# Third scores ahead of the out projection and the turning of h, in 29 of 64 steps of a transformer kernel

## The chip, the cores and the metric

The kernel runs on one core of a Trainium2 chip. The metric is the device time of one execution in microseconds (us), as the median of three executions. Five engines run their own instruction streams and meet at semaphores: TensorE (PE, its weight loads shown apart as PEld), VectorE (DVE), ScalarE (ACT), GpSimd (POOL) and SyncE (SP), which issues most of the DMAs.

## The reference

The input is 16 sequences of 256 tokens with 128 channels. A modulated layer norm and a wavelet mixer with linear attention come first; then four transformer layers, each with attention (16 query heads on 4 key heads, head size 64, causal) and a mixture of 8 experts of which every token uses two:

```python
for l in range(L):                       # L = 4
    res = x
    h = _rms(x, ln1_w[l])
    h = _attention(h, wq[l], wk[l], wv[l], wo[l], cos, sin, causal_bias)
    x = jnp.clip(res + h, -100.0, 100.0)
    res = x
    h = _rms(x, ln2_w[l])
    h = _moe(h, wr[l], wg[l], wu[l], wd[l])
    x = jnp.clip(res + h, -100.0, 100.0)
```

Inside `_attention`: q and k are projected and rotated by position, scores are scaled and masked, a softmax follows, the probabilities weigh v, and `wo` projects the result out.

## The kernel before, in words

After a prologue of some 243 us the kernel runs 64 **steps**, one for each sequence in each layer (16 sequences, 4 layers), and ends with the experts of the last eight sequences. A step `it` works on three sequences at once: attention of `it`; the rest of the attention, the out projection and the routing of `it - 1`; and the norm and the q and k projections of `it + 1`. The experts run in blocks of eight sequences, cut into 42 half steps, which are laid into the eight **places** (0 to 7) of later steps. Steps 0 to 8 have none at any place. In each later group of eight, the steps with remainder 0 and 7 have none, the step with remainder 1 has them at places 4 to 7 only, and the one with remainder 6 at places 0 to 5; the others have all eight. So place 3 is empty in steps 0 to 9, 15 to 17, 23 to 25, 31 to 33, 39 to 41, 47 to 49, 55 to 57 and 63: 29 steps, called light steps here. In all of them place 2 is empty too.

Nothing schedules at run time. Each engine's order is written out by hand in a loop over the steps, and the loops of PE and DVE have to name the same order, since they share PSUM banks. In a light step, between places 1 and 3, it is:

- PE: `scores(it, 1)` (L759), `attend(it - 1, 3)` (transposes L784, then the products with v, L802 and L804), `project_v(it)` (L841), `project_out(it - 1)` (L852), `turn_h(it + 1)` (L817, two transposes of the normed rows z), `scores(it, 2)` (L759), and after place 3 `project_qk(it + 1)` for outputs 0 and 1 (L832 to L834), `turn_routed(it - 1)` (L861) and output 2. After place 4 come `attend(it, 0)`, `route_logits` (L870), `scores(it, 3)`, outputs 3 and 4, `attend(it, 1)`, `route_ranks`.
- DVE: `mask_and_max(it, 1)`, `invert(it, 0)`, `copy_o(it - 1, 3)` (L1606), `update_x(it - 1)` (L1612, L1615), `low_h(it + 1)` (L1585), `mask_and_max(it, 2)` (four heads, each L1591 and L1593, then L1597), `invert(it, 1)` (L1602), `rope(it + 1)` for outputs 0 to 2 (L1572, two for each).
- ACT: `exps(it, 1)` (L1055), `copy_v`, `scale_rows(it + 1)`, `square_routed(it - 1)` (L1077), `copy_h(it + 1)` (L1072, L1073), `scale_routed`, and later `exps(it, 2)` behind `copy_logits`.
- POOL: `scatter(it - 2)` (L1299), `root`, `normalise(it, 0)` (L1308), `root_routed(it - 1)`, `normalise(it, 1)`, `low_piece`, `rope_adds` of outputs 0 to 2 (L1323), `normalise(it, 2)`.

`normalise(it, q)` divides the exponentials of the group of heads `q` after DVE's `invert`; `attend(it, q)` waits for it. `rope_adds` waits for a DMA that SP issues after `rope`.

**Banks.** Scores, out projection and q and k projections take turns in a ring of four PSUM banks (the S ring), numbered by `number_slots` in PE's order. A product may start when the slot four before it has been read:

```python
at_least(pe, "s_free", S_AT["out", it] - S_RING + 1)   # in project_out
```

`project_out` waits for this and, ahead of it, for `copy_o` of the last group. `project_qk` waits for `h_lo_ready` and for its own slot.

The chain that the new sequence's h takes is: out projection done, `update_x`, squares on ACT, `copy_h` on ACT (behind the squares in ACT's order), `low_h` on DVE, `project_qk`.

Of the kernel before, what the change touches and what calls it, by code (L numbers as in the profile page):

```python
# [128 lines left out]
def number_slots(half_steps):  # L129

    s, t, u = {}, {}, {}

    def moe(b, hs):
        m = hs // 2
        g = b * PT + m
        if hs % 2 == 0:
            if m < PT:
                u["rows", g] = len(u)
            if m > 0:
                u["gated", g - 1] = len(u)  # L140
        else:
            if m < PT:
                u["gate", g, 0] = len(u)
                u["gate", g, 1] = len(u)
            if m > 0:
                t["y", g - 1] = len(t)

    def place(it, p):
        if (it, p) in half_steps:
            moe(*half_steps[it, p])  # L150

    def scores(it, q):
        for i in range(4):
            s["head", it, q, i] = len(s)

    def attend(it, q):
        for i in range(4):
            t["probs", it, q, i] = len(t)
        u["o", it, q] = len(u)

    def qk(it, outputs):
        for m in outputs:
            s["qk", it, m] = len(s)

    for it in range(-1, NIT + 1):
        now, coming, old = 0 <= it < NIT, it + 1 < NIT, it >= 1
        if now:
            scores(it, 0)
        place(it, 0)
        if old:  # L170
            attend(it - 1, 2)
        place(it, 1)
        if now:
            scores(it, 1)
        if old:
            attend(it - 1, 3)
        if now:
            t["v", it] = len(t)
        place(it, 2)
        if old:  # L180
            s["out", it - 1] = len(s)
        if coming:
            t["h", it + 1] = len(t)
        if now:
            scores(it, 2)
        place(it, 3)
        if coming:
            qk(it + 1, range(2))
        if old:
            t["routed", it - 1] = len(t)  # L190
        if coming:
            qk(it + 1, range(2, N_QK1))
        place(it, 4)
        if now:
            attend(it, 0)
        if old:
            t["logits", it - 1] = len(t)
        place(it, 5)
        if now:
            scores(it, 3)  # L200
        place(it, 6)
        if coming:
            qk(it + 1, range(N_QK1, N_QK))
        if now:
            attend(it, 1)
        if old:
            t["ranks", it - 1] = len(t)
        place(it, 7)
    for hs in range(HS):
        moe(NB - 1, hs)  # L210
    return s, t, u


def bass_program(nc, I, out):
    ctx = ExitStack()
    with ctx:
# [207 lines left out]
        half_steps = half_step_places()  # L424
# [251 lines left out]
        def _(pe):  # L676
# [268 lines left out]
            def place(it, p):  # L945
                if (it, p) in half_steps:
                    moe(*half_steps[it, p])

            phase_done(pe, 0)
            for it in range(-1, NIT + 1):  # L950
                now, coming, old = 0 <= it < NIT, it + 1 < NIT, it >= 1
                if now:
                    scores(it, 0)
                place(it, 0)
                if old:
                    attend(it - 1, 2)
                place(it, 1)
                if now:
                    scores(it, 1)
                if old:  # L960
                    attend(it - 1, 3)
                if now:
                    project_v(it)
                place(it, 2)
                if old:
                    project_out(it - 1)
                if coming:
                    turn_h(it + 1)
                if now:
                    scores(it, 2)  # L970
                place(it, 3)
                if coming:
                    project_qk(it + 1, range(2))
                if old:
                    turn_routed(it - 1)
                if coming:
                    project_qk(it + 1, range(2, N_QK1))
                place(it, 4)
                if now:
                    attend(it, 0)  # L980
                if old:
                    route_logits(it - 1)
                place(it, 5)
                if now:
                    scores(it, 3)
                place(it, 6)
                if coming:
                    project_qk(it + 1, range(N_QK1, N_QK))
                if now:
                    attend(it, 1)  # L990
                if old:
                    route_ranks(it - 1)
                place(it, 7)
# [374 lines left out]
        def _(dve):  # L1368
# [235 lines left out]
            def copy_o(it, q):  # L1604
                u_is_full(dve, ("o", it, q))
                V.tensor_copy(oT[:, 2 * q:2 * q + 2, :].rearrange("p a b -> p (a b)"), psum[:, u_bank(("o", it, q)), :]) \  # L1606
                    .then_inc(sem("u_free"), 1)
# [100 lines left out]
            def place(it, p):  # L1708
                if (it, p) in half_steps:
                    moe(*half_steps[it, p])  # L1710
# [3 lines left out]
            for it in range(-1, NIT + 1):  # L1714
                now, coming, old = 0 <= it < NIT, it + 1 < NIT, it >= 1
                if now:
                    mask_and_max(it, 0)
                if old:
                    invert(it - 1, 3)
                place(it, 0)  # L1720
                if old:
                    copy_o(it - 1, 2)
                if coming and it + 1 >= B:
                    combine(it + 1)
                place(it, 1)
                if now:
                    mask_and_max(it, 1)
                    invert(it, 0)
                if old:
                    copy_o(it - 1, 3)  # L1730
                place(it, 2)
                if old:
                    update_x(it - 1)
                if coming:
                    low_h(it + 1)
                if now:
                    mask_and_max(it, 2)
                    invert(it, 1)
                place(it, 3)
                if coming:  # L1740
                    rope(it + 1, range(N_QK1))
                place(it, 4)
                if now:
                    copy_o(it, 0)
                if old:
                    choose(it - 1)
                place(it, 5)
                if now:
                    mask_and_max(it, 3)
                    invert(it, 2)  # L1750
                place(it, 6)
                if coming:
                    rope(it + 1, range(N_QK1, N_QK))
                if now:
                    copy_o(it, 1)
                if old:
                    route(it - 1)
                place(it, 7)
# [58 lines left out]
```

How the kernel before makes its waits and increments, by code:

```python
        def phase_done(eng, k):  # L410
            eng.wait_ge(sem("phase_end"), PH * (k + 1))
# [1 line left out]
        def at_least(eng, name, n):  # L414
            if n > 0:
                eng.wait_ge(sem(name), n)
# [19 lines left out]
        def s_is_full(eng, key):  # L437
            eng.wait_ge(sem("s_full"), S_AT[key] + 1)
# [1 line left out]
        def t_is_full(eng, key):  # L440
            eng.wait_ge(sem("t_full"), T_AT[key] + 1)
# [1 line left out]
        def u_is_full(eng, key):  # L443
            eng.wait_ge(sem("u_full"), U_AT[key] + 1)
# [1 line left out]
        def s_was_read(eng, key):  # L446
            eng.wait_ge(sem("s_free"), S_AT[key] + 1)
# [1 line left out]
        def t_was_read(eng, key):  # L449
            eng.wait_ge(sem("t_free"), T_AT[key] + 1)
# [1 line left out]
        def u_was_read(eng, key):  # L452
            eng.wait_ge(sem("u_free"), U_AT[key] + 1)
# [34 lines left out]
        @block.sync  # L488
# [19 lines left out]
            def load_wv(l):  # L508
                load(wv, I["wv"][l], "wv_in")
            def load_wo(l):
                load(wo, I["wo_blocks"][l].rearrange("(c p) n -> p c n", p=P), "wo_in")
            load_wv(0)
            load_wo(0)
            load(wr, I["L0_ffn_wr"].rearrange("l h n -> h l n"), "wr_in")
            sp.wait_ge(sem("zeros_ready"), 1)
            for rows in rows_in + rows_out:
                for q in range(ZERO_PIECES):
                    sp.dma_start(zero_piece(rows, q), zeros).then_inc(sem("rows_zeroed"), 16)
            for h in range(2):
                sp.wait_ge(sem("x1_ready"), h + 1)
                sp.dma_start(x1_kept[:, half(h), :], x1[:, half(h), :]).then_inc(sem("x1_stored"), 16)
            def load_piece(it):
```

## Time and profile before

| | us |
|---|---|
| median of 3 executions | 3266.18 |
| lowest, highest | 3264.12, 3277.45 |
| the profiled execution | 3285.71 |
| its span, first to last instruction | 3283.9 |

In the profiled execution PE is busy for 80% of the span, DVE 67%, ACT 61%, POOL 57%. The mean granted TensorE clock is 0.919 of full speed: it stands at one of two levels, 1.2 or 2.4 GHz. Steps without expert work take 35.3 to 41 us, steps with it at all places 46.7 to 50 us. Times in rows are counted from the start of the span; "[x <-y]" behind a row is the idle time of its engine before it and what ended it. Matmuls are recorded as two instructions each where the operands are f32.

### The profile page before, as it was taken

The page shows a single profiled execution, that of the slowest core. Times are in us where ns is not written, and L with a number is a line of the kernel's source. Part 1 is how long each engine was busy: PE and PEld are TensorE (multiplying, and loading weights), DVE is VectorE, ACT ScalarE, POOL GpSimd, SP SyncE. Part 2 cuts the span into 40 slices and gives each one's busy share as a digit, 9 for nine tenths or more (in the row PEclk, how much of TensorE's full clock was granted, in tenths as well). Part 3 has the DMA queues.
Part 4 walks back from the last instruction along what each step waited for, and adds up shares of the span by engine and source line. Part 5 has one row for each costly group of instructions (what it writes and reads, how often), then busy time and mean ns, then how long its engine had stood idle before and what let it go on. Part 6 is the DMA issues. An engine that isn't in the chain of part 4 may idle for free.

```text
span 3283.9 us, 66162 instructions
## 1 busy us (share of the span) xinstructions
PE 2618.0 (80%) x20406; PEld 2095.5 (64%) x20406; DVE 2207.6 (67%) x8164; ACT 1996.6 (61%) x7080; POOL 1861.3 (57%) x1662
## 2 busy tenths in 40 slices
PE   5317887898889987899789987898889978998572
PEld 2316666777667766777667766777677766776462
DVE  6686676666777667776676767677676666765343
ACT  3017677667667666666666766676666766666220
POOL 0026676545666667655765666566766576555403
PEclk9659999999999999999999999999999999999665
DMA  9211122556246642654256633654266624652574
GB/s 373 118 46 65 68 78 86 181 177 198 71 161 212 206 137 80 222 192 154 77 189 228 212 106 116 201 194 139 74 214 218 200 76 145 201 193 89 164 240 128
DMA packets 287022, 511.54 MB, mean 156 GB/s; under 512 B 39969, under 2 KB 159297, under 8 KB 286145
## 3 DMA queue, kind: packets, MB, share of 16 engines
q1 hardware_dynamic: 270288, 473.72, 42.6%
q0 software_dynamic: 16384, 33.59, 3.3%
q8 instruction: 167, 2.74, 0.4%
q14 instruction: 183, 1.49, 0.2%
HBM read 316.58 MB, written 106.69 MB: 129 GB/s over the span
## 4 chain that ended last, share of the span: by engine, by line
PE 43%; DVE 19%; ACT 12%; POOL 11%; issue 7%; SPq 3%; another core or an unknown queue 3%; DMA 2%; DVEq 0%; POOLq 0%
PE psum L784 6%; PE psum L802 6%; DVE arena L1572 5%; ACT arena L1055 4%; PE psum L759 4%; PE psum L852 4%; POOL arena L1308 4%; ACT arena L1063 3%; PE psum L804 3%; POOL arena L1275 2%; DVE arena L1593 2%; PE psum L902 2%; PE psum L832 2%; POOL rows_in L1299 2%
## 5 line engine op out<-in xcount | busy, mean ns | idle before, releaser
L1055 ACT ACTIVATE arena<-arena 128x128 f32<-128x128 f32 (+1 forms) x2048 | 902.3, 446 | 53.4 <-DVE arena L1597 47.5
L1308 POOL TENSOR_TENSOR arena<-arena 128x512 f32<-128x512 f32 (+1 forms) x512 | 743.6, 1472 | 208.4 <-DVE arena L1602 208.3
L1323 POOL TENSOR_TENSOR arena<-arena 128x512 f32<-128x512 f32 x320 | 401.6, 1282 | 491.6 <-DMA arena<-arena 491.3
L784 PE MATMUL psum<-arena 128*128 128x128 f32 x3072 | 478.1, 294 | 225.5 <-ACT arena L1063 154.9
L1063 ACT COPY arena<-psum 128x384 f32<-128x384 f32 x1024 | 447.5, 482 | 312.7 <-PE psum L784 217.4
L784 PEld LDWEIGHTS psum<-arena 128*128 128x128 f32 x3072 | 347.5, 147 | 341.0 <-ACT arena L1063 214.5
L759 PE MATMUL psum<-arena 64*128 64x128 f32 (+1 forms) x4096 | 419.8, 342 | 12.7 <-DVE arena L1593 7.0
L1593 DVE CUSTOM_DVE_ANT_0 arena<-psum,arena 128x256 f32<-128x256 f32 x1024 | 429.3, 419 | 0.0
L1606 DVE COPY arena<-psum 128x512 f32<-128x512 f32 x256 | 176.4, 689 | 347.3 <-PE psum L804 314.2
L1572 DVE TENSOR_TENSOR arena<-psum,arena 128x512 f32<-128x512 f32 x640 | 390.8, 675 | 1.9 <-PE psum L834 1.8
L1055 ACT ACTIVATION_READ_ACCUMULATOR arena<-arena 128x1 f32 x2048 | 389.9, 190 | 0.0
L802 PE MATMUL psum<-arena 128*64 128x256 f32 x2048 | 355.3, 428 | 35.7 <-DVE xT_lo L1683 30.2
L759 PEld LDWEIGHTS psum<-arena 64*128 64x128 f32 x4096 | 301.3, 190 | 55.7 <-issue 26.2
L1591 DVE CUSTOM_DVE_ANT_0 arena<-psum,arena 128x128 f32<-128x128 f32 x1024 | 292.4, 286 | 31.3 <-PE psum L759 17.0
L1299 POOL DMA_INDIRECT rows_in<-arena x256 | 259.4, 1013 | 75.3 <-issue 69.3
L852 PE MATMUL psum<-arena 128*128 128x128 f32 x2048 | 247.3, 279 | 27.6 <-issue 27.5
L852 PEld LDWEIGHTS psum<-arena 128*128 128x128 f32 x2048 | 240.3, 196 | 37.0 <-issue 36.5
L832 PE MATMUL psum<-h_hi,wqk_hi 128*128 128x256 f32 x640 | 197.1, 308 | 69.2 <-DVE arena L1593 52.6
L804 PEld LDWEIGHTS psum<-arena 128*64 128x64 f32 x2048 | 160.3, 150 | 91.6 <-issue 26.7
L1275 POOL DMA_INDIRECT arena<-rows_out,arena x192 | 189.1, 985 | 52.3 <-issue 52.3
L804 PE MATMUL psum<-arena 128*64 128x128 f32 x2048 | 215.1, 290 | 0.0
L1689 DVE SCALAR_TENSOR_TENSOR arena<-arena,psum 128x512 f32<-128x512 f32 x160 | 108.0, 675 | 149.2 <-ACT arena L1138 122.9
(199 smaller groups left out, 5440.5 us busy)
## 6 DMA issues: line engine op xcount, KB each, us to landing
gu<-gu_kept SPq DMA_DIRECT2D x320, 512.0 KB
wd<-wd_kept SPq DMA_DIRECT2D x320, 256.0 KB
arena<-arena SPq DMA_DIRECT2D x128, 384.0 KB, 3.0
arena<-arena SPq DMA_DIRECT2D x128, 256.0 KB
arena<-rows_in SPq DMA_DIRECT2D x320, 64.0 KB
rows_out<-arena SPq DMA_DIRECT2D x320, 64.0 KB
rows_in<-arena SPq DMA_DIRECT2D x34, 512.0 KB, 8.0
rows_out<-arena SPq DMA_DIRECT2D x34, 512.0 KB, 7.1
```

Source lines behind the costliest of these rows:

```text
L759: return T.matmul(psum[:, s_bank(("head", it, q, i)), cols], QKT[par][r, 2 + 2 * q + i // 2, rows * P:(rows + 1) * P], QKT[par][r, q // 2, ...
L784: mm = T.transpose(psum[:, t_bank(key), j * P:(j + 1) * P], probs[:, q, i, j * P:(j + 1) * P], ident)
L802: return T.matmul(psum[r, bank, c0:c0 + S], v[:, 0, kv], pt[:, 0:S], start=True, stop=False, skip_group_check=True)
L804: return T.matmul(psum[r, bank, c0 + P:c0 + S], v[:, 1, kv], pt[:, S:S + P], start=False, stop=True, skip_group_check=True)
L852: mm = T.matmul(psum[:, s_bank(("out", it)), t * P:(t + 1) * P], oT[:, c, t * P:(t + 1) * P], wo[:, c, :], start=(c == 0), stop=(c == NH / ...
L1055: ins = A.activation(a, a, ACT.Exp, bias=negmax[:, q, k:k + 1], accum_out=rowsum[:, q, k:k + 1])
L1063: A.copy(probsT[:, 4 * (q % 2) + i, :], psum[:, t_bank(key), 0:3 * P]).then_inc(sem("t_free"), 1)
L1299: G.indirect_dma_start(rows_in[b % 2], bass.IndirectOffsetOnAxis(place_of[:, it % B * ST + t, j:j + 1], 0), z2[:, it % 2, t, :], None).the ...
L1308: ins = G.tensor_tensor(a, a, r[:, :, t:t + 1].broadcast_to([P, 4, P * (t + 1)]), ALU.mult)
L1323: G.tensor_tensor(keys_and_queries(it, u), keys_and_queries(it, u), turned_part[:, u, :], ALU.add) \
L1572: return V.tensor_tensor(dst.rearrange("p (i s) -> p i s", i=2), psum[:, s_bank(("qk", it, u)), :].rearrange("p (i s) -> p i s", i=2), tab ...
L1593: V.tensor_tensor_reduce(probs[:, q, i, P:3 * P], psum[:, s_bank(key), P:3 * P], mask, SCALE, -3.0e38, ALU.add, ALU.max, rowmax[:, q, 2 * ...
```

## The change

In the three places that set the order (the numbering of the slots, PE's loop and DVE's loop), steps whose place 3 is empty get `scores(it, 2)` before `project_out(it - 1)` and `turn_h(it + 1)`. On DVE `mask_and_max(it, 2)` and `invert(it, 1)` come before `update_x(it - 1)` and `low_h(it + 1)`. Steps with expert work at place 3 keep their order. ACT, POOL and SP keep theirs everywhere. No instruction is added or removed.

```diff
@@ number_slots @@
+        free = (it, 3) not in half_steps
+        if now and free:
+            scores(it, 2)
         if old:
             s["out", it - 1] = len(s)
         if coming:
             t["h", it + 1] = len(t)
-        if now:
+        if now and not free:
             scores(it, 2)
@@ TensorE's loop @@
+                free = (it, 3) not in half_steps
+                if now and free:
+                    scores(it, 2)
                 if old:
                     project_out(it - 1)
                 if coming:
                     turn_h(it + 1)
-                if now:
+                if now and not free:
                     scores(it, 2)
@@ VectorE's loop @@
                 if old:
                     copy_o(it - 1, 3)
+                free = (it, 3) not in half_steps
+                if now and free:
+                    mask_and_max(it, 2)
                 place(it, 2)
+                if now and free:
+                    invert(it, 1)
                 if old:
                     update_x(it - 1)
                 if coming:
                     low_h(it + 1)
-                if now:
+                if now and not free:
                     mask_and_max(it, 2)
                     invert(it, 1)
```

PE in a light step, from the v projection to the first q and k projection, before (`L852` is the out projection, `L817` the turning of h, `L759` the scores):

```order
L841 MATMUL psum<-arena 128x256 x2
L852 MATMUL psum<-arena 128x128 x16
L817 MATMUL psum<-arena 128x128 x2
L759 MATMUL psum<-arena 128x128 x2
L759 MATMUL psum<-arena 128x256 x2
L759 MATMUL psum<-arena 128x128 x2
L759 MATMUL psum<-arena 128x256 x2
L832 MATMUL psum<-h_hi,wqk_hi 128x256
```

and after (every line number is 3 higher):

```order
L844 MATMUL psum<-arena 128x256 x2
L762 MATMUL psum<-arena 128x128 x2
L762 MATMUL psum<-arena 128x256 x2
L762 MATMUL psum<-arena 128x128 x2
L762 MATMUL psum<-arena 128x256 x2
L855 MATMUL psum<-arena 128x128 x16
L820 MATMUL psum<-arena 128x128 x2
L835 MATMUL psum<-h_hi,wqk_hi 128x256
```

The eight products of the third scores left the place between `turn_h` and `project_qk`, where nothing stands now, and stand ahead of the out projection.

DVE at the same place, from `copy_o` (L1606) on, before; L1612 and L1615 are `update_x`, L1585 `low_h`, and the mask of the first head follows:

```order
L1606 COPY arena<-psum 128x512
L1612 TENSOR_TENSOR arena<-arena,psum 128x256
L1615 TENSOR_SCALAR arena<-arena 128x256
L1585 TENSOR_TENSOR h_lo<-arena,h_hi 128x256
L1591 ISA arena<-psum,arena 128x128
```

and after, the end of that piece (line numbers 6 higher): the last head's mask, the negation L1603, `invert` L1608, `update_x`, `low_h`, and at once `rope` (L1578):

```order
L1599 ISA arena 128x1
L1603 TENSOR_SCALAR arena<-arena 128x8
L1608 RECIPROCAL arena<-arena 128x8
L1618 TENSOR_TENSOR arena<-arena,psum 128x256
L1621 TENSOR_SCALAR arena<-arena 128x256
L1591 TENSOR_TENSOR h_lo<-arena,h_hi 128x256
L1578 TENSOR_TENSOR arena<-psum,arena 128x512 x6
```

The whole third mask moved from behind `low_h` to before `update_x`.

## Rows read from the trace of the kernel before

**Rows 1.** The page: busy time and share of each engine; the chain that ended last.

```profile
PE 2618.0 (80%) x20406; PEld 2095.5 (64%) x20406; DVE 2207.6 (67%) x8164; ACT 1996.6 (61%) x7080; POOL 1861.3 (57%) x1662
...
PE 43%; DVE 19%; ACT 12%; POOL 11%; issue 7%; SPq 3%; another core or an unknown queue 3%; DMA 2%; DVEq 0%; POOLq 0%
```

**Rows 2.** Timeline of step 4: start us, length us, engine, line, operation, operands, count.

```profile
398.92 0.69 DVE L1606 COPY arena<-psum 128x512 f32<-128x512 f32 x1 [3.28 <-PE psum L804]
...
399.71 3.81 PE L852 MATMUL psum<-arena 128*128 128x128 f32 x32 [0.68 <-issue]
...
403.36 0.38 PE L817 MATMUL psum<-arena 128*128 128x128 f32 x2
403.56 0.42 DVE L1612 TENSOR_TENSOR arena<-arena,psum 128x256 f32<-128x256 f32 x1 [3.95 <-PE psum L852]
...
403.67 1.58 PE L759 MATMUL psum<-arena 64*128 64x128 f32 x16
...
404.94 0.45 ACT L1072 ACTIVATE h_hi<-psum,arena 128x256 fp32r<-128x256 f32 x1
...
405.79 0.42 DVE L1585 TENSOR_TENSOR h_lo<-arena,h_hi 128x256 fp32r<-128x256 f32 x1 [1.48 <-ACT arena L1073]
406.13 0.28 DVE L1591 CUSTOM_DVE_ANT_0 arena<-psum,arena 128x128 f32<-128x128 f32 x1
...
406.68 0.08 DVE L1593 DVE_READ_ACCUMULATOR2_ANT arena<- 128x1 f32 x1
...
406.91 0.36 PE L832 MATMUL psum<-h_hi,wqk_hi 128*128 128x256 f32 x1 [1.66 <-DVE arena L1593]
...
408.66 1.83 DVE L1572 TENSOR_TENSOR arena<-psum,arena 128x512 f32<-128x512 f32 x3
```

**Rows 3.** Timeline of the end of step 4: POOL, and then PE in step 5.

```profile
415.86 3.77 POOL L1323 TENSOR_TENSOR arena<-arena 128x512 f32<-128x512 f32 x3 [2.35 <-DMA arena<-arena]
419.57 2.92 POOL L1308 TENSOR_TENSOR arena<-arena 128x512 f32<-128x512 f32 x2
...
422.55 0.66 PE L784 MATMUL psum<-arena 128*128 128x128 f32 x4 [0.17 <-POOL arena L1308]
```

**Rows 4.** Timeline of PE and DVE in step 3, the out projection and what ran before.

```profile
359.49 1.13 PE L841 MATMUL psum<-arena 128*128 128x256 f32 x4
362.75 5.44 PE L852 MATMUL psum<-arena 128*128 128x128 f32 x32 [2.13 <-issue]
...
361.95 0.69 DVE L1606 COPY arena<-psum 128x512 f32<-128x512 f32 x1 [4.24 <-remote]
```

**Rows 5.** Windows: stretch, length, busy PE, PEld, DVE, ACT, POOL, granted clock (PEclk), DMA share, GB/s; 6 us from `project_qk`'s start.

```profile
371.58:377.58 6.00, 5.76 (x50) 4.80 (x50) 5.40 (x21) 2.88 (x6) 4.09 (x3) 1.00 0.00 0
2702.81:2708.81 6.00, 4.60 (x35) 3.85 (x36) 5.33 (x20) 2.58 (x7) 4.81 (x5) 1.00 0.09 22
```

**Rows 6.** Windows, 6 us behind PE waits of 2.61, 3.00 and 2.42 us.

```profile
283.45:289.45 6.00, 5.76 (x47) 4.61 (x48) 0.77 (x2) 5.16 (x22) 2.68 (x4) 1.00 0.00 0
857.42:863.42 6.00, 5.75 (x32) 3.79 (x32) 3.88 (x24) 4.59 (x19) 4.87 (x6) 0.72 0.12 45
1302.28:1308.28 6.00, 5.77 (x32) 3.81 (x32) 3.84 (x23) 5.12 (x21) 4.85 (x6) 0.72 0.11 44
```

**Rows 7.** Windows, 6 us from the out projection's start, behind waits of 2.13 and 2.09 us.

```profile
362.75:368.75 6.00, 6.00 (x40) 5.83 (x42) 0.49 (x2) 1.02 (x3) 2.23 (x2) 0.72 0.01 3
508.85:514.85 6.00, 5.54 (x50) 4.92 (x50) 0.71 (x2) 2.44 (x9) 2.78 (x4) 1.00 0.00 0
```

**Rows 8.** Timeline of PE, outputs 3 and 4 and `attend(it, 1)`, in steps 3 and 40.

```profile
380.38 0.36 PE L832 MATMUL psum<-h_hi,wqk_hi 128*128 128x256 f32 x1 [0.85 <-DVE arena L1593]
...
383.80 0.65 PE L802 MATMUL psum<-arena 128*64 128x256 f32 x4
...
1998.81 0.44 PE L832 MATMUL psum<-h_hi,wqk_hi 128*128 128x256 f32 x1 [2.95 <-DVE arena L1593]
...
2003.73 0.65 PE L802 MATMUL psum<-arena 128*64 128x256 f32 x3
```

**Rows 9.** Windows of whole steps: 11 and 13 (experts at all places).

```profile
661.06:709.10 48.04, 43.97 (x353) 36.04 (x352) 31.77 (x125) 32.70 (x118) 23.71 (x21) 0.96 0.56 187
757.07:803.94 46.87, 42.58 (x352) 35.10 (x351) 31.56 (x125) 32.57 (x117) 23.72 (x21) 1.00 0.59 192
```

## The prediction, made before the changed kernel ran

> **What bounds the kernel now.** I read the page first, for the balance of the engines: PE is the busiest with 80% of the span and holds 43% of the chain that ended last, but DVE, ACT and POOL hold 42% of it together [rows 1]. So no engine is full; the work passes from hand to hand, and a change of order counts by what it does to the chain in a step. Then I read the timeline of a light step at full clock, step 4 [rows 2]. PE waits for `copy_o` of the last group of heads (DVE, 398.92), starts the out projection at 399.71, turns h until 403.36 + 0.38 = 403.74, and does the third scores (403.67, 1.58 us) while h goes from `update_x` (403.56) over ACT (404.94) to `low_h` (405.79 + 0.42 = 406.21). `project_qk` starts at 406.91, 1.66 us after the scores ended. What it waited for last is not h but a bank: output 0's slot is four behind the third scores' first head, and DVE masks that head only behind `low_h`, from 406.13 to 406.68 + 0.08. The windows were read last, for the granted clock behind such waits.
>
> **The change, term by term.** 29 steps change; steps 0 and 63 lack a neighbour, so 27 full ones count. Nothing is added or removed, so every term is a matter of place.
>
> *The start of the out projection.* Its slot now stands four behind the third scores' first head. Hence it waits for `copy_o` and for DVE to mask that head behind it. The mask of one head takes 406.76 - 406.13 = 0.63 us, and PE starts 0.15 us behind it, at 406.91 [rows 2]. Before, PE followed `copy_o` by 0.1 us; now by some 0.75. Cost: +0.65 us in each step. The scores themselves fit into PE's idle time ahead: 0.68 us of it in step 4 [rows 2], 2.13 in step 3 [rows 4], so in steps like 4 their first result comes at the earliest some 0.9 us after the v projection and the mask starts about 0.3 later. I take +0.65 to +0.95.
>
> *The start of `project_qk`.* The h chain keeps its length, since `update_x` finds DVE free: the third mask (2.5 us) and `invert` are over before the 3.81 us of the out projection are. But behind `low_h` nothing is left to wait for: the slot four before is the third scores' second head, long read. PE can start at about 406.25 instead of 406.91 [rows 2]: -0.66. The two terms cancel: 0 to +0.3 us a step, I take +0.15, which is +4 us for 27 steps.
>
> *`rope` of outputs 0 to 2.* DVE began it at 408.66 because mask and `invert` came before [rows 2]. Now it can follow output 0 directly, about 0.83 us (seven spacings of 0.12) behind the start of `project_qk`, near 407.9: -0.8 us. POOL's `rope_adds` waits 2.35 us for the DMA behind that work, and `normalise` of the third group follows it and ends at 422.49, where PE has waited only 0.17 us [rows 3]. So at most 0.17 us of the 0.8 is worth anything there, up to 0.5 in other steps; next comes PE's own product. I take 0, and -0.3 a step (-8 us) as its far bound.
>
> *The wait of PE before `project_qk`.* Here lies the largest term. The 1.58 us of scores that lay between `turn_h` and `project_qk` are gone. PE is idle from 403.74 to 406.25 in the times of step 4, so 2.5 us where it was idle 1.66 [rows 2]. As such this costs nothing, since h sets the end. But the granted clock hangs on PE's idle time. Behind the old wait of 1.66 us the clock stayed at 1.00 in all nine light steps that I looked at; the first and the last are shown [rows 5]. Behind seven waits of 2.42 to 3.00 us it fell to the lower level six times (0.72 in the mean of the next 6 us) and stayed once, after 2.61; three of the seven are shown [rows 6]. Behind the five waits of 2.09 to 2.17 us ahead of an out projection it fell four times; one of each kind is shown [rows 7]. The new wait lies between these two kinds, so I take 3 in 4: 20 falls of the clock in 27 steps, with 13 (half) and 25 as ends.
>
> *The price of a fall.* It now hits work that PE does without a pause: 18 projections, then `attend(it, 0)`, the logits and the fourth scores. Three rows price it. An out projection takes 5.44 us with a fall in it [rows 4] and 3.81 without [rows 2]: 1.63. From output 3 to the products with v it is 2003.73 - 1998.81 = 4.92 us at the lower level against 383.80 - 380.38 = 3.42 [rows 8]: 1.50. Whole steps that differ by one such fall take 48.04 and 46.87 [rows 9]: 1.17. I take 1.4. Sum: 20 x 1.4 = +28 us, ends 13 x 1.2 = +16 and 25 x 1.6 = +40.
>
> Here a page of the Trainium skill puts a price of its own: "TensorE: Matmul & The Clock Gate", Terms, counts the penalty as the throttled time multiplied by (1 - K/N), half of it at the lower level. Step 11 has a mean clock of 0.96 over 48.04 us, which is 0.08 x 48 = 3.8 us at the lower level, so by the page 1.9 us against the 1.17 us that the step lost; with 1.9 for each of the falls the term would be 38 us. The whole step decides here, since part of a fall lies on waits.
>
> *Falls that go.* Ahead of the out projection PE now has the scores to do, so waits of 2.13 us shrink to about 2.13 + 0.75 - 1.58 = 1.3 us. The four falls there (steps 3, 16, 31 and 57) should go: -4 x 1.6 = -6 us.
>
> *Steps 0 and 63.* Step 0 has no out projection and gains the 0.66 us; step 63 has no `project_qk` and loses 0.7 us: 0.
>
> **Sum:** +4 + 28 - 6 = +26 us. The profiled execution took 3285.7 us, 19.5 (0.6%) over the median 3266.2; the difference carries over to the median. I round to **3291 us**, +25 us or +0.8%. What a measurement of this kernel can tell from no change is about 0.5%, or 16 us: below 3250 counts as faster, above 3282 as slower.
>
> **The rivals.**
>
> *A. The clock holds, little changes.* The new wait has busy work on both sides, as the wait of 2.61 us had, behind which the clock stayed [rows 6]; or falls only change places with those that steps have anyway. Then +4 - 6, less up to 8 us for the earlier `rope`: 3256 to 3266, about 3262. With half of the falls (+16) it would still be 3276. For it: one in seven rows. Against it: the other six, and four in five at a shorter wait. Chance 0.28, with everything from 3250 to 3282.
>
> *B. Faster: the early `rope` pulls the POOL chain.* `rope_adds` and the `normalise` behind it come 0.8 us earlier. Where PE waits on POOL for the third group and ACT's copies wait behind PE, up to 0.5 us a step comes back: 27 x 0.5 = 14 us, and 6 us of old falls go. That is 3266 - 20 = 3246 us. It decides only if no new fall eats it, and if POOL and not PE ends the wait at 422.55; the row shows 0.17 us between them [rows 3]. Chance 0.08.
>
> *C. Much slower: the first mask comes late.* While POOL issues its scatter, PE's results reach others late: in step 3 `copy_o` starts at 361.95, though the v projection behind its product was issued at 359.49 [rows 4]. If the release of the third scores is held likewise, by another 0.5 to 1.4 us in the 20 or so light steps with a scatter there, the out projection and all behind it come as much later: 20 x 1 = +20 on top of the sum, 3311 us. Against it: in step 3 the lateness ends with `copy_o`, ahead of which no mask could run anyway. Chance 0.12.
>
> *D. As summed*, 3283 to 3303: chance 0.52.
>
> **How the numbers follow.** The predicted time is D's. Faster by over 0.5%: B, 0.08. Within 0.5%: A, 0.28. Slower: C and D, 0.64. The range reaches into A's low end and to C, with some 0.1 left out on either side: 3254 to 3312.
>
> **What would show it.** In the changed trace a light step at full clock should have: scores directly behind the v projection; the out projection 0.75 us behind the start of the mask that follows `copy_o`; an idle time of 2.5 us before L835, ended by `low_h`; `rope` some 0.9 us behind L835. The windows behind that wait should show 0.72 in about 20 of 27 cases, the mean clock should go from 0.919 to about 0.91, and the light steps with a fall should be 1.2 to 1.6 us longer than before, the steps with experts unchanged at 46.7 to 48.1. I am wrong if the wait is shorter than 2 us, if the clock stays up behind it, or if steps with such a fall are no longer than those without.

## The result, and the profile after

The changed kernel takes 3349.36 us (median of 4 executions, 3346.28 to 3353.18); the kernel before takes 3267.0 us (4 executions, the three of above among them, 3264.12 to 3277.45). The ratio is 1.0247, with a 95% interval of 1.0221 to 1.0272: **82 us slower**, 2.5%. The forecast was 3291 us, 25 slower, with 3312 as the upper end. The sign was right, the size was not, and most of the difference is a term that the forecast does not have.

The page of the changed kernel, first the span, then busy time and the chain that ended last:

```profile
span 3349.1 us, 66162 instructions
...
PE 2650.1 (79%) x20406; PEld 2124.2 (63%) x20406; DVE 2249.7 (67%) x8164; ACT 1999.4 (60%) x7080; POOL 1863.4 (56%) x1662
...
PE 49%; DVE 19%; ACT 10%; POOL 8%; issue 7%; SPq 3%; DMA 2%; another core or an unknown queue 2%; DVEq 0%; POOLq 0%
```

Against [rows 1], PE is busy 32 us more and DVE 42 us more, with the same instructions. PE's surplus goes with the granted clock: 0.911 in the mean, 0.919 before. DVE does the same instructions in more time; 39 of its 42 us are found below, in one group of short instructions. The chain has moved from POOL (11% to 8%) to PE (43% to 49%).

Counted in the two traces, the 28 light steps before step 63 went from 1128.6 to 1199.4 us, and the other 35 from 1628.2 to 1618.9. All of the loss lies in the changed steps. (The traces differ by 65 us and not by 82, since the profiled execution of before was 19 us over its median.) The timeline of step 4, PE from the v projection (L844) over scores (L762), out projection (L855) and turning of h (L820) to `project_qk` (L835), and DVE from `copy_o` (L1612) over the first head's mask (L1597), `update_x` (L1618) and `low_h` (L1591) to `rope` (L1578):

```profile
404.71 1.13 PE L844 MATMUL psum<-arena 128*128 128x256 f32 x4
405.77 1.58 PE L762 MATMUL psum<-arena 64*128 64x128 f32 x16
407.82 3.81 PE L855 MATMUL psum<-arena 128*128 128x128 f32 x32 [0.47 <-DVE arena L1599]
411.47 0.38 PE L820 MATMUL psum<-arena 128*128 128x128 f32 x2
414.38 0.58 PE L835 MATMUL psum<-h_hi,wqk_hi 128*128 128x256 f32 x1 [2.53 <-DVE h_lo L1591]
```

```profile
406.44 0.69 DVE L1612 COPY arena<-psum 128x512 f32<-128x512 f32 x1 [3.09 <-remote]
407.04 0.28 DVE L1597 CUSTOM_DVE_ANT_0 arena<-psum,arena 128x128 f32<-128x128 f32 x1
...
411.67 0.42 DVE L1618 TENSOR_TENSOR arena<-arena,psum 128x256 f32<-128x256 f32 x1 [2.01 <-PE psum L855]
...
413.90 0.43 DVE L1591 TENSOR_TENSOR h_lo<-arena,h_hi 128x256 fp32r<-128x256 f32 x1 [1.48 <-ACT arena L1079]
416.13 3.77 DVE L1578 TENSOR_TENSOR arena<-psum,arena 128x512 f32<-128x512 f32 x6 [1.81 <-PE psum L837]
```

The order is the one announced: the out projection now waits for a head's mask (L1599), and the wait before `project_qk` is 2.53 us, ended by `low_h`, where it was 1.66 and ended by a mask [rows 2]. The windows (columns as in [rows 5]) over 6 us from `project_qk` on, first of step 4, then of step 3:

```profile
414.38:420.38 6.00, 5.76 (x34) 5.25 (x36) 3.77 (x6) 3.17 (x8) 4.56 (x3) 0.74 0.00 0
377.71:383.71 6.00, 5.76 (x50) 4.81 (x50) 3.72 (x7) 3.53 (x8) 4.54 (x3) 1.00 0.03 11
```

Behind the same wait, 2.53 us in both, the clock fell in step 4 and stayed in step 3. It fell behind 17 of the 27 waits.

**What the forecast did not have** comes 8 us later in step 4. DVE's `choose` (the two best experts of each token: MAX8 L1627 to L1639), and POOL's `rope_adds` (L1329):

```profile
422.46 0.24 DVE L1627 MAX8 arena<-arena 128x8 f32<-128x8 f32 x2
...
423.21 0.17 DVE L1634 CAST arena<-arena 128x4 f32<-128x4 uint32 x1
423.42 1.36 DVE L1637 TENSOR_TENSOR arena<-arena 128x16 f32<-128x16 f32 x2
424.81 1.19 DVE L1639 TENSOR_TENSOR chosen_bf<-arena 128x16 bf16<-128x16 f32 x1
```

```profile
423.48 3.73 POOL L1329 TENSOR_TENSOR arena<-arena 128x512 f32<-128x512 f32 x3 [4.54 <-DMA arena<-arena]
```

A DVE operation on sixteen columns takes 0.17 us as a rule (the median of L1637 and of L1639). Here a pair of such operations takes 1.36 us and the next 1.19, while POOL adds operands of 512 columns, 3.73 us for three. The whole `choose` lasts 3.54 us instead of 1.42. The mask of the fourth scores stands behind it on DVE, and outputs 3 and 4 wait for that mask's banks; PE waits 2.97 us there, where [rows 8] have 0.85 in step 3 of before, and the clock is down behind that wait too, as the timeline and the window from there show:

```profile
426.70 0.36 PE L835 MATMUL psum<-h_hi,wqk_hi 128*128 128x256 f32 x1 [2.97 <-DVE arena L1599]
```

```profile
426.70:432.70 6.00, 6.00 (x40) 4.96 (x40) 4.15 (x18) 1.92 (x4) 3.42 (x3) 0.72 0.12 48
```

How much this is in all is seen in the groups by line: busy us in total and mean ns of one, for the 128 and the 64 small operations at the end of `choose`, first after:

```profile
L1637 DVE TENSOR_TENSOR arena<-arena 128x16 f32<-128x16 f32 x128 | 34.7, 312 | 2.2
L1639 DVE TENSOR_TENSOR chosen_bf<-arena 128x16 bf16<-128x16 f32 x64 | 27.6, 431 | 2.2
```

and before:

```profile
L1631 DVE TENSOR_TENSOR arena<-arena 128x16 f32<-128x16 f32 x128 | 18.8, 189 | 2.2
L1633 DVE TENSOR_TENSOR chosen_bf<-arena 128x16 bf16<-128x16 f32 x64 | 13.2, 205 | 2.2
```

I call a `choose` of over 1.8 us a **collision**. Of the 64 executions of `choose` there are 2 before, with 4.2 us over the usual 1.42 in all, and 18 after, with 43.2 us; 14 of the 18 stand in steps with a fall.

### The profile page after: what moved, and what is told of

It reads as the page before. It is cut to its first block, busy times and chain, and to the rows that moved or that the text cites. A ratio compares the mean times of both kernels' runs of the same rounds, so it can differ in the third digit from the quotient of the medians.

```text
span 3349.1 us, 66162 instructions
## 1 busy us (share of the span) xinstructions
PE 2650.1 (79%) x20406; PEld 2124.2 (63%) x20406; DVE 2249.7 (67%) x8164; ACT 1999.4 (60%) x7080; POOL 1863.4 (56%) x1662
## 4 chain that ended last, share of the span: by engine, by line
PE 49%; DVE 19%; ACT 10%; POOL 8%; issue 7%; SPq 3%; DMA 2%; another core or an unknown queue 2%; DVEq 0%; POOLq 0%
PE psum L787 8%; PE psum L805 6%; PE psum L762 6%; PE psum L855 4%; DVE arena L1578 4%; ACT arena L1061 4%; PE psum L807 3%; ACT arena L1069 3%; POOL arena L1314 3%; PE psum L835 2%; PE psum L905 2%; DVE arena L1599 2%; PE psum L837 2%; PE psum L836 2%; POOL arena L1281 2%
## 5 line engine op out<-in xcount | busy, mean ns | idle before, releaser
L1329 POOL TENSOR_TENSOR arena<-arena 128x512 f32<-128x512 f32 x320 | 401.8, 1283 | 543.3 <-DMA arena<-arena 543.2
L1612 DVE COPY arena<-psum 128x512 f32<-128x512 f32 x256 | 176.8, 690 | 390.0 <-PE psum L807 361.8
L1599 DVE CUSTOM_DVE_ANT_0 arena<-psum,arena 128x256 f32<-128x256 f32 x1024 | 429.4, 419 | 0.0
L1578 DVE TENSOR_TENSOR arena<-psum,arena 128x512 f32<-128x512 f32 x640 | 395.5, 680 | 48.2 <-PE psum L837 41.2
L762 PE MATMUL psum<-arena 64*128 64x128 f32 (+1 forms) x4096 | 417.6, 342 | 7.6 <-POOL arena L1329 5.8
L762 PEld LDWEIGHTS psum<-arena 64*128 64x128 f32 x4096 | 300.7, 190 | 56.3 <-issue 26.6
L1597 DVE CUSTOM_DVE_ANT_0 arena<-psum,arena 128x128 f32<-128x128 f32 x1024 | 292.4, 286 | 35.6 <-PE psum L762 27.8
L835 PE MATMUL psum<-h_hi,wqk_hi 128*128 128x256 f32 x640 | 213.0, 333 | 121.1 <-issue 51.4
L855 PE MATMUL psum<-arena 128*128 128x128 f32 x2048 | 242.9, 276 | 14.2 <-DVE arena L1599 12.2
L855 PEld LDWEIGHTS psum<-arena 128*128 128x128 f32 x2048 | 235.2, 193 | 24.9 <-issue 24.9
L835 PEld LDWEIGHTS psum<-h_hi,wqk_hi 128*128 128x128 f32 x640 | 137.4, 215 | 138.2 <-issue 111.0
```

What stands on the lines that cost most here:

```text
L762: return T.matmul(psum[:, s_bank(("head", it, q, i)), cols], QKT[par][r, 2 + 2 * q + i // 2, rows * P:(rows + 1) * P], QKT[par][r, q // 2, ...
L835: T.matmul(out, wqk_hi[:, cols], h_hi, start=True, stop=False)
L855: mm = T.matmul(psum[:, s_bank(("out", it)), t * P:(t + 1) * P], oT[:, c, t * P:(t + 1) * P], wo[:, c, :], start=(c == 0), stop=(c == NH / ...
L1329: G.tensor_tensor(keys_and_queries(it, u), keys_and_queries(it, u), turned_part[:, u, :], ALU.add) \
L1578: return V.tensor_tensor(dst.rearrange("p (i s) -> p i s", i=2), psum[:, s_bank(("qk", it, u)), :].rearrange("p (i s) -> p i s", i=2), tab ...
L1599: V.tensor_tensor_reduce(probs[:, q, i, P:3 * P], psum[:, s_bank(key), P:3 * P], mask, SCALE, -3.0e38, ALU.add, ALU.max, rowmax[:, q, 2 * ...
```

## The experiments

Theory: of the 82 us, most needs the collision of `choose` with `rope_adds`, the rest is the falls of the clock and the later out projection. Rivals: the falls alone, at a higher price than forecast; and the order alone. Two edits tell them apart. **Fill** gives PE four idle products in the new wait, to see whether the clock then stays up. The **wait of POOL** holds `rope_adds` until `choose` is done, so that they can't collide. All kernels compute the whole result.

**Fill**, on the changed kernel, in the light steps:

```diff
+            def busy(it, n):
+                at_least(pe, "s_free", S_AT["qk", it, 0] - S_RING + 1)
+                for k in range(n):
+                    T.matmul(psum[:, s_bank(("qk", it, 0)), 0:S], ident, mask, start=True, stop=True)
...
                 if coming:
                     turn_h(it + 1)
+                if now and coming and free:
+                    busy(it + 1, 4)
```

> The changed kernel, and in each light step four more products of 256 columns (identity by mask, into the bank that output 0 overwrites) on PE between the turning of h and project_qk, about 1.7 us of work in the idle 2.5 us. Nothing reads them. Theory 1, the clock starts it all: the wait before project_qk no longer brings the clock down, choose no longer runs into rope_adds, and most of the 82 us goes: 3265 to 3285 us. Theory 2, the collision of DVE's choose with POOL's rope_adds comes from the earlier rope and not from the clock: 3320 us or more, choose still over 3 us long in some 18 steps.

Measured: 3287.4 us (10 executions), ratio to before 1.0041 [1.0017, 1.0065]. None of the 27 waits has a fall behind it; their median is 0.85 us. But collisions went with the falls, from 18 to 5. So this run alone doesn't separate the two.

**The wait of POOL**, on the changed kernel:

```diff
+                if old and now:
+                    pool.wait_ge(sem("chosen_ready"), it)
                 if coming:
                     rope_adds(it + 1, range(N_QK1))
```

> The changed kernel, but POOL waits for choose of the same step before rope_adds of outputs 0 to 2, in every step. Theory 1 (falls of the clock, and the collision as their consequence) and theory 2 agree that the collisions go, here at 2.1 to 3.1 us in 18 steps: 40 us back, 3305 to 3315 us, with the falls of the clock left. If the stretched choose costs nothing because something else ends the step, or POOL's later start costs as much, it stays at 3340 to 3355.

Measured: 3288.0 us (6 executions), ratio 1.0055 [1.0033, 1.0077], so 61 us less than the changed kernel, and below the 3305 to 3315 expected. No collision is left, but 16 of the 27 waits still have a fall behind them. One line of the source view (shortest, median and longest in ns) shows the cause gone; here the small operation stands on L1639:

```profile
L1639 DVE TENSOR_TENSOR arena<-arena x128: 167/174/178, 307.0 to 3057.9; 128x16 f32<-128x16 f32 x128
```

The same view of the changed kernel has 1292 ns as the longest:

```profile
L1637 DVE TENSOR_TENSOR arena<-arena x128: 160/174/1292, 307.0 to 3125.5; 128x16 f32<-128x16 f32 x128
```

**Both edits:**

> Both additions. Theory 1: as with the filling alone, 3260 to 3285, since with the clock up there is little left to collide. If the two causes are independent, it is lower than the filling alone by what the wait alone gave, some 30 to 40 us.

Measured: 3268.1 us (10 executions), ratio 0.9992 [0.9971, 1.0012]. Against the wait alone that is 20 us for 16 falls: **1.25 us a fall**, whatever the fillers cost included. The two intervals leave 10 to 30 us open. The one profile of the wait alone puts a fall higher: from `project_qk` to the next step's start the 16 light steps with a fall take 17.20 us in the mean, the other 11 take 15.24. With neither falls nor collisions the changed order ties with the kernel before.

The two causes do not simply add up. POOL's wait gives 61 us while the falls are there, and 3287.4 - 3268.1 = 19 us once the fillers have taken them away; the fillers give 62 us while there can be collisions, and 20 without. So some 42 us need both: a fall makes `choose` late, and the late `choose` runs into `rope_adds`.

**The wait of POOL on the kernel before**, since that has collisions of its own:

> The kernel before, with the same wait of POOL for choose. In its trace choose is stretched in 2 steps only (40 and 56, 3.5 against 1.4 us), so it should gain 4 us at most, and lose nothing in light steps, where choose ends 0.85 us before rope_adds starts: 3258 to 3270. Slower than 3275 would mean that the wait itself costs in steps with experts.

Measured: 3256.5 us (8 executions), ratio 0.9954 [0.9929, 0.998]: 14 us faster than the kernel before, where 4 at most were expected. The trace of before has only 4.2 us of excess in `choose`, so where the rest of the 14 comes from is not shown. Taken as measured, 14 of the 61 us that the wait brings to the changed kernel are not the change's doing, and the changed order with both edits (3268.1) is 12 us slower than the old order with the wait; the intervals leave 1 to 22 us open. I book these 12 as the price of the order, but the two profiles do not place them there: the 28 light steps take 1109.3 us with both edits and 1116.4 in the old order with the wait, the other 35 steps 1621.7 and 1610.9.

**Does a POOL add alone hold `choose`?** On the kernel before, in light steps, POOL adds the same 512 columns once more at the moment at which `choose` runs:

```diff
+        probe_out = arena.take(512)
...
+                if old and now and (it, 3) not in half_steps:
+                    pool.wait_ge(sem("gap_ready"), it)
+                    c = consts[:, K_COS:K_COS + 512]
+                    G.tensor_tensor(probe_out, c, c, ALU.add)
                 if coming:
                     rope_adds(it + 1, range(N_QK1))
```

> The kernel before, with one more add of 128 x 512 on POOL in each light step with routing (28 of them), started when choose has begun (its gap is written) and over before rope_adds would start; its result is not used. It prices a collision of POOL's adds with choose by itself, with the old order and no new idle time of PE. Theory: DVE's small operations wait until POOL's add is over, choose takes some 1 to 1.3 us longer in 28 steps, and what follows it too: +28 to +40 us, 3298 to 3310. If the long choose of the changed kernel only went along with the falls of the clock and POOL's adds do not hold DVE, choose stays at 1.4 us and the time within 8 us of before.

Measured: 3226.6 us (10 executions) against 3212.6 of before on this chip, ratio 1.0046 [1.0026, 1.0066]: +14 us, less than the 28 to 40 expected. The timeline of DVE in `choose`, and of POOL, shows the hold in this kernel on another instruction, the cast:

```profile
411.31 0.82 DVE L1633 CAST arena<-arena 128x4 f32<-128x4 uint32 x1
412.17 0.26 DVE L1636 TENSOR_TENSOR arena<-arena 128x16 f32<-128x16 f32 x2
```

```profile
411.07 1.04 POOL L1347 TENSOR_TENSOR arena<-arena 128x512 f32<-128x512 f32 x1 [0.59 <-DVE arena L1628]
```

The cast takes 0.82 us for 0.17, until POOL's add ends at 412.11. An add of the same size on unrelated operands is enough. There are 30 collisions with 52.4 us of excess. The undisturbed kernel has 16 with 36.6 us on another chip on which it takes about the same time (below); it was not profiled on this one. If this chip is like that one, the probe added 16 us of excess for 14 us of time, and it cost less than expected because most was being paid already, and because one add held `choose` for 0.66 us in steps 1 to 9 and not for 1 to 1.3.

**Fillers on the kernel before, with POOL's wait**: idle products ahead of `attend(it - 1, 3)` and of the out projection, where falls were left.

```diff
+                if old and light and it >= 14:
+                    t_is_free(("probs", it - 1, 3, 0))
+                    busy(t_bank(("probs", it - 1, 3, 0)), 1 if it % HB == 0 else 3)
                 if old:
                     attend(it - 1, 3)
...
+                if old and light:
+                    at_least(pe, "s_free", S_AT["out", it - 1] - S_RING + 1)
+                    busy(s_bank(("out", it - 1)), 1)
```

> The kernel before with POOL's wait (3256.5 us), and filling products on PE in the waits that light steps have left: one ahead of each out projection, and from step 14 on three ahead of attend of group 3 (one where the step's number divides by 8). If falls of the clock cost 1.2 to 1.6 us each, the 10 to 15 falls that stand behind these waits go and it takes 3235 to 3248. If the fillings delay what they stand before, it is 3256 or slower.

Measured: 3174.8 us (4 executions), ratio 0.9879 [0.9839, 0.992]. The time at the lower level inside the loop is 82 us. What of the gain is the wait's and what the fillers' is told by the pair on the third chip, below.

**Scatter later.** To see whether POOL's scatter is what makes PE's results late (rival C), the scatter of steps 2 to 8 was issued behind `root_routed`, with POOL's wait:

```diff
-                if it >= 2:
+                if it >= 2 and not it <= 8:
                     scatter(it - 2)
...
+                if 2 <= it <= 8:
+                    scatter(it - 2)
```

> The kernel before with POOL's wait, and in steps 2 to 8 POOL issues the scatter behind the routed root instead of at the step's start. If PE's results come late because of the running scatter, copy_o of the last group starts right behind the product with v in these seven steps (it lags 0.9 to 2.4 us in six of them), and the out projection begins some 1 us sooner: 3249 to 3254 us. If the lag has another cause, it stays, and the time is 3254 to 3259.

Measured: 3185.9 us (6 executions), ratio 0.9921 [0.9893, 0.9948], slower than the kernel with the scatter in its place (3174.8, with fillers besides). The run doesn't answer its question: on this chip `copy_o` starts 0.12 us behind the start of the v projection in steps 2 to 9 even with the scatter in its old place. It brought 7 stretched executions of `choose` back, 13.2 us in all, though `rope_adds` waited. Now POOL's `normalise` (L1308) and `low_piece` (L1316, 768 columns), which come before that wait, lay beside `choose` and held its subtraction of two columns (L1627), 0.16 us otherwise; DVE, then POOL:

```profile
335.65 2.23 DVE L1627 TENSOR_TENSOR arena<-arena 128x2 f32<-128x2 f32 x1
```

```profile
333.19 2.91 POOL L1308 TENSOR_TENSOR arena<-arena 128x512 f32<-128x512 f32 x2
336.05 1.80 POOL L1316 TENSOR_TENSOR w_lo<-arena,w_hi 128x768 fp32r<-128x768 f32 x1
```

The subtraction starts 0.4 us before `low_piece`, while the last multiplication of `normalise` still runs, and ends with `low_piece` at 337.9: it was held across two POOL instructions, and so in all seven steps (1.77 to 2.23 us). So POOL's wait has to stand ahead of whatever is late enough to meet `choose`, and `rope_adds` is only what meets it in the kernel before.

**A third chip, before and after again.** The kernel before took 3270 us on the chip of the first four experiments, 3213 on that of the next three. (The set of the changed kernel, with 3267 for before, is counted to the first chip.) So both kernels ran once more, beside the two with POOL's wait:

> The kernel before, unchanged, with a profile of its own on the chip of this set, since the set before this one had a chip on which it took 3212.6 us and not 3270. Where this chip is the faster kind, the profile shows which part of the steps is shorter, and how often choose is stretched (2 times in the first profile). Ratio 1.00.

> The changed kernel on the same chip. If collisions and falls are its cost on any chip, the ratio is 1.020 to 1.028 again, choose is over 3 us long in 15 to 20 steps, and the clock falls behind the 2.5 us wait in 14 to 20 of 27. If the kernel before has such collisions of its own on this chip, the ratio is nearer to 1.

> The kernel before with POOL's wait, on the same chip: ratio 0.993 to 0.998 as in the first set; lower by as many collisions as the kernel before has here, some 2 us for each.

> With the filling products as well: 10 to 25 us below the wait alone on the same chip, if 10 to 15 falls of the clock go. If the gain of the run before (ratio 0.988) was the chip's and the wait's, it is level with the wait alone.

| | us, median | ratio to before, 95% | collisions, excess us | falls behind the wait of `project_qk` |
|---|---|---|---|---|
| before again | 3207.4 | 1.0008 [0.9983, 1.0033] | 16, 36.6 | 3 of 27 |
| after again | 3270.1 | 1.0182 [1.0148, 1.0216] | 26, 51.5 | 26 of 27 |
| before, POOL waits | 3166.7 | 0.9872 [0.9848, 0.9895] | 0 | 0 |
| the same with fillers | 3173.9 | 0.9900 [0.9876, 0.9924] | 0 | 0 |

The change costs 1.8% here and 2.5% on the first chip. On this one the kernel before already has 16 collisions, which fits; that they are the reason was not tested. The wait of POOL brings it 1.3%, and the fillers nothing: 3173.9 with them, 3166.7 without, though the time at the lower level falls from 120 to 96 us. **The kernel before with POOL's wait is the best version**, faster than before and after on both chips where it ran (0.9954 and 0.9872).

This chip also gives the cleanest measure of the order, since `copy_o` is hardly ever late on it (0.16 us behind the start of the v projection in the mean of before, 1.28 on the first chip). In the mean of the 27 light steps, the out projection starts 2.72 us behind `copy_o`'s start in the changed kernel, 0.83 in the kernel before with POOL's wait; `project_qk` 2.96 us behind `turn_h` against 3.51.

## Where the prediction was right, and where it failed

**The sum, by the runs of the first chip.**

| term | forecast, us | measured, us | from |
|---|---|---|---|
| later out projection, earlier `project_qk`, old falls gone | +4 - 6 | +12 | both edits against before with the wait |
| new falls | +28 | +20 | wait alone against both edits |
| collisions, net of those that before has | not in the sum | +47 | 3349.4 - 3288.0 = 61, less 3270.4 - 3256.5 = 14 |
| sum | +26 | +79 | 3349.4 - 3270.4; against the 3267.0 measured beside the changed kernel it is 82 |

The three measured terms are differences along one path between the same two kernels, so their sum closes by itself and confirms nothing. They also hold for this order of taking causes away only: with the fillers first, the falls and what they bring are 62 us, and the collisions that are left 19.

*The missing term.* The step that failed is "`rope` of outputs 0 to 2", which asked only what an earlier `rope` could gain on POOL, took 0 and set a far bound of -8: no price above zero. It did not ask what DVE does while `rope_adds` runs. The numbers were in the trace of before. PE's wait of 2.95 us in step 40 [rows 8], from which I priced a fall, stands behind one of the two collisions of before: `choose` takes 3.52 us in that step. And in step 4, `rope_adds` starts at 415.86 [rows 3], and `choose` ended at 415.01, a row that I had not drawn:

```profile
414.83 0.17 DVE L1633 TENSOR_TENSOR chosen_bf<-arena 128x16 bf16<-128x16 f32 x1
```

A margin of 0.85 us held the two apart. Further on in the same step the negation behind the fourth mask, 0.17 us in the median, took 1.16 us beside these additions:

```profile
417.26 1.16 DVE L1597 TENSOR_SCALAR arena<-arena 128x8 f32<-128x8 f32 x1
```

The change shrinks the margin from both sides. Counted from the start of `project_qk` in step 4:

| | `choose` starts | `rope_adds` start |
|---|---|---|
| before | 413.59 - 406.91 = 6.68 | 415.86 - 406.91 = 8.95 |
| both edits | 411.15 - 404.46 = 6.69 | 412.88 - 404.46 = 8.42 |
| after, with a fall | 422.46 - 414.38 = 8.08 | 423.48 - 414.38 = 9.10 |

The rows of the kernel with both edits, where `rope_adds` had its DMA last:

```profile
404.46 0.38 PE L840 MATMUL psum<-h_hi,wqk_hi 128*128 128x256 f32 x1 [0.80 <-DVE h_lo L1600]
...
411.15 0.24 DVE L1636 MAX8 arena<-arena 128x8 f32<-128x8 f32 x2
...
412.40 0.17 DVE L1648 TENSOR_TENSOR chosen_bf<-arena 128x16 bf16<-128x16 f32 x1
...
412.88 3.78 POOL L1336 TENSOR_TENSOR arena<-arena 128x512 f32<-128x512 f32 x3 [3.87 <-DMA arena<-arena]
```

The earlier `rope` takes 0.53 us of the margin, so it does happen as forecast, as a loss instead of a gain. The fall takes the rest: it delays what PE must do before `choose` (projections, `attend`, logits) by 1.4 us, but `rope_adds`, which needs only the first outputs and a DMA, by 0.7. Both shares show in the runs: the kernel before has 2 collisions, the changed order 5 without falls and 18 with them. A collision then costs more than its own length (61 us for 43.2), and the traces point at the late fourth mask: PE waits for it and the clock falls once more, as at 426.70 in step 4. The clock fell there in 9 of the 27 light steps of the changed kernel, in 2 of before, and in none once POOL waits. No run took this last link away by itself. The counts are of one execution each, the times medians of several.

Here a page of the Trainium skill would have pointed the right way. In "SBUF — State Buffer", section "Who interferes with whom", it says that a VectorE instruction with two SBUF inputs contends with a GpSimd instruction that reads SBUF, and that whoever comes second is blocked until the other ends. The trace agrees: L1637 and L1639 compare and add two operands in SBUF, and each ends with one of POOL's additions (1.2 to 1.3 us), while the masks from 425.92 to 427.2 us, with one input in PSUM, take their usual 0.28 and 0.42 us beside the third addition. The cast of the probe, with one input in SBUF, was held too (0.82 us for 0.17); the page allows this for copies and casts in a mode that uses both ports. The subtraction that was held across two POOL instructions is more than the page's rule says; no run here shows why.

*The falls*: right in mechanism, and near in size where nothing collides. 17 of 27 on this chip against 20, at 1.25 us each against 1.4; on the third chip 26 of 27, which is past the upper end of 25. That 3 in 4 lies between the two chips is luck, since the forecast rested on the waits of one. What it missed is that a fall here also makes `choose` late. The Trainium skill's price, half of the time at the lower level ("TensorE: Matmul & The Clock Gate", Terms), comes out too high again: the kernel with the wait alone has 232 us at that level in the loop, the one with both edits 136, which makes 48 us by the page, an estimate, against 20 measured.

*The old falls ahead of the out projection* went, as forecast. In step 3 it had taken 5.44 us [rows 4]; in the changed kernel it takes 3.81, and no light step is longer:

```profile
371.15 3.81 PE L855 MATMUL psum<-arena 128*128 128x128 f32 x32 [0.91 <-DVE arena L1599]
```

*The start of `project_qk`*: right in step 4. It comes 2.91 us behind `turn_h` in step 4 against 3.55 before, -0.64 for a forecast of -0.66; in the mean of the 27 steps it is 3.13 against 3.57.

*The start of the out projection* was mis-sized. The forecast had +0.65 to +0.95 over before; measured is +0.6 where `copy_o` is late, as in step 4 (407.82 - 406.44 = 1.38 against 0.79), and +1.9 where it is not. The mean of the 27 steps went from 0.84 to 1.90 us. Step 1 of the changed kernel shows why, PE and then DVE:

```profile
288.49 1.13 PE L844 MATMUL psum<-arena 128*128 128x256 f32 x4
289.56 1.58 PE L762 MATMUL psum<-arena 64*128 64x128 f32 x16
291.30 1.46 PE L855 MATMUL psum<-arena 128*128 128x128 f32 x11 [0.17 <-DVE arena L1599]
```

```profile
288.61 0.69 DVE L1612 COPY arena<-psum 128x512 f32<-128x512 f32 x1 [4.73 <-PE psum L807]
290.51 0.29 DVE L1597 CUSTOM_DVE_ANT_0 arena<-psum,arena 128x128 f32<-128x128 f32 x1 [1.21 <-PE psum L762]
```

I had put the mask 0.9 + 0.3 us behind the v projection. It starts 290.51 - 288.49 = 2.02 us behind it: 1.07 until the scores start and 0.95 from there to the mask. The out projection then can't start earlier than 2.8 us behind the v projection, where before 0.97 was enough. I had taken step 4, in which `copy_o` is late by 1 us anyway, for the pattern. With 0.64 back, such a step loses 1.26 us on the way to `project_qk` (third chip, 9.45 against 8.19 us from the v projection) and not 0.15. On the first chip, with both edits against before with the wait, the same way is 9.75 against 8.95 us, which is 22 us in 27 steps; of that 12 show in the whole time, and where the rest is won back was not settled.

*The steps with experts* were to stay the same; the 35 unchanged steps became 9 us shorter in all (1628.2 to 1618.9), 0.3 us each.

**The rivals.** A (the clock holds) is out by the falls, B (faster) by the time. (A's side figure of 3276 us for half of the falls should be 3266 + 4 - 6 + 16 = 3280; it stays within its bound of 3282.) C has no support: in step 4 `copy_o` is late (406.44, 1.73 us behind the start of the v projection), but the mask follows it at once, at 407.04. Its time, 3311, was the nearest, by luck. Why results of PE reach DVE late on the first chip and not on the others was not settled.

The forecast for light steps, 1.2 to 1.6 us longer with a fall, is where the error is seen first. Step 4 took 35.3 us before; the window over it in the changed kernel has 41.38:

```profile
391.62:433.00 41.38, 33.10 (x259) 26.33 (x256) 25.22 (x109) 26.41 (x100) 26.78 (x23) 0.88 0.21 77
```

## What to carry to other kernels

When an edit shifts one engine against another, look at what DVE and POOL do side by side at the new times, above all at short DVE operations with both operands in SBUF: a margin of 0.85 us, once lost, cost some 47 us of run time together with the falls that used it up. A wait that holds the long operations behind the short ones gained 0.5% and 1.3% here, net of what it costs. Work moved ahead of a wait is not free for filling idle time: its result now has to pass a second engine before the wait can end, and that way has to be measured in a step where nothing else is late.

## What the runs showed of the hardware

- DVE operations on 16 columns took up to 1.29 us instead of 0.17 while POOL added 512 columns (1.28 us each). The masks, which read PSUM, ran unchanged beside the same additions. Casts of four columns (up to 1.27 us) and a negation of eight (1.16 us), with one input in SBUF, were held too. A subtraction of two columns took 1.77 to 2.23 us, from within one POOL instruction to the end of the next.
- Behind one and the same wait of 2.5 to 2.6 us the clock fell 16 or 17 times in 27 on one chip and 26 times on another, and in neighbouring steps of one execution it fell and held.
- The kernel before took 3270, 3213 and 3207 us on three chips. The 35 unchanged steps, most with experts, make the difference (1628 us in the first trace, 1538 in that of the third chip), not the light ones (1129 and 1164). The same change cost 2.5% on the first chip and 1.8% on the third.
- Taking 24 us of time at the lower level away with idle products gained nothing (3173.9 against 3166.7 us), while 96 us taken away in the changed kernel with POOL's wait gained 20.
